# Two attention stages of a six-stage transformer kernel: first-block scores of four heads in one product, maxima added to the query rows on VectorE, and a shifted order of projection and value products

## The reference

```
x = x + 0.5 * L0_ffn(layernorm(x))      # 32 gated experts, 8 chosen, and a shared one
x = x + L0_attn(layernorm(x))           # "attn0": 16 heads of 8, causal softmax
x = x + 0.5 * L0_ffn(layernorm(x))
x = x + 0.5 * L1_ffn(layernorm(x))      # 8 experts of 512, 2 chosen
x = x + L1_attn(layernorm(x))           # "attn1": 16 heads of 8, relu scores / their sum
x = x + 0.5 * L1_ffn(layernorm(x))

# attn0, for each of 8 batches, S = 512, H = 16, HD = 8
scores  = einsum('bhqd,bhkd->bhqk', Q, K) / sqrt(8);  scores = where(k > q, -1e6, scores)
attn    = einsum('bhqk,bhkd->bhqd', softmax(scores), V) @ Wo + bo
# attn1, inside it a residual and a layer norm of its own
w       = relu(einsum('bhqd,bhkd->bhqk', q, k) / sqrt(8));  w = w / (sum(w) + 1e-6)
y       = x + einsum('bhqk,bhkd->bhqd', w, v) @ w_out + b_out;  out = layernorm(y)*gamma + beta
```

## Time and profile before

| | |
|---|---|
| median of 3 runs | 2064.63 us (2064.27 to 2064.72) |
| profiled execution | 2066.3 us, its span 2064.3 us |
| busy over the span | PE 1985.8 us (96%), DVE 1632.7 (79%), ACT 1200.7 (58%), POOL 930.1 (45%) |
| chain that ended last, by engine | PE 64%, DVE 11%, issue 11%, POOL 9%, ACT 3% |
| attn0 | first exponential at 347.8, last at 707.6 us; a loop chunk 45.78 us |
| attn1 | first scores at 1416.4, last at 1677.4 us; loop chunks 31.9 to 34.7 us |

### The profile page before, as it was taken

One profiled execution on the slowest core, in us unless ns is written; L12 is line 12 of the kernel. 1 busy time (PEld: TensorE's weight loads), 2 busy tenths in 40 slices (PEclk: granted clock), 3 DMA queues, 4 the chain that ended last, 5 costly groups with the idle time before them and its releaser, 6 DMA issues.

```text
span 2064.3 us, 44740 instructions
## 1 busy us (share of the span) xinstructions
PE 1985.8 (96%) x10752; PEld 1438.8 (70%) x10752; DVE 1632.7 (79%) x3337; ACT 1200.7 (58%) x1736; POOL 930.1 (45%) x904
## 2 busy tenths in 40 slices
PE   6999998999999999999999999998999999999998
PEld 4777776666666677777877888874333357787787
DVE  7777777777777577777588888886777788888887
ACT  6667664555555577676554445445767764454544
POOL 4665663333332366666544444442122334444444
PEclk9999999999999999999999999999999999999999
DMA  6333343333232243444311111114233301111112
GB/s 210 101 122 113 108 120 112 98 97 96 82 91 82 55 130 118 130 129 114 112 37 47 41 46 46 45 43 138 84 130 104 120 28 46 47 46 41 41 51 72
DMA packets 120701, 179.29 MB, mean 87 GB/s; under 512 B 33840, under 2 KB 38576, under 8 KB 120496
## 3 DMA queue, kind: packets, MB, share of 16 engines
q1 hardware_dynamic: 120624, 178.37, 29.3%
HBM read 147.10 MB, written 31.20 MB: 86 GB/s over the span
## 4 chain that ended last, share of the span: by engine, by line
PE 64%; DVE 11%; issue 11%; POOL 9%; ACT 3%; DVEq 1%; POOLq 1%; DMA 0%; SPq 0%; ACTq 0%
PE pair L397 14%; PE pair L399 13%; PE pair L398 13%; POOL h_lo L1364 6%; PE bank L651 5%; PE pair L740 3%; PE bank L629 3%; PE pair L762 3%; PE pair L823 2%; PE bank L397 2%; PE bank L399 1%; PE bank L398 1%; DVE rmax L1188 1%; DVE h_hi L1131 1%; POOL rstd L1284 1%
## 5 line engine op out<-in xcount | busy, mean ns | idle before, releaser
L1370 POOL TENSOR_TENSOR h_lo<-hid,h_hi 128x512 fp32r<-128x512 f32 x256 | 335.5, 1311 | 410.4 <-ACT h_hi L920 410.1
L397 PE MATMUL pair<-xnT_hi,w_hi 128*128 (+1 forms) x1040 | 420.0, 404 | 2.6 <-DVE prod L1110 1.3
L1364 POOL TENSOR_TENSOR h_lo<-hid,h_hi 128x512 fp32r<-128x512 f32 x256 | 332.3, 1300 | 194.6 <-ACT h_hi L886 193.4
L399 PE MATMUL pair<-xnT_hi,w_lo 128*128 (+1 forms) x1040 | 407.7, 392 | 0.0
L398 PE MATMUL pair<-xnT_lo,w_hi 128*128 (+1 forms) x1040 | 407.4, 392 | 0.0
L915 ACT ACTIVATE hid<-pair,bias 128x512 f32<-128x512 f32 x256 | 176.6, 690 | 315.5 <-PE pair L399 273.8
L397 PE MATMUL pair<-h_hi,w_hi 128*128 128x512 f32 x784 | 311.5, 397 | 14.5 <-DVE h_lo L1133 6.2
L399 PE MATMUL pair<-h_hi,w_lo 128*128 128x512 f32 x784 | 306.5, 391 | 0.0
L398 PE MATMUL pair<-h_lo,w_hi 128*128 128x512 f32 x784 | 305.9, 390 | 0.0
L1131 DVE TENSOR_SCALAR h_hi<-pair,nb 128x512 fp32r<-128x512 f32 x256 | 191.2, 747 | 69.8 <-PE pair L399 67.1
L938 ACT ACTIVATE probs<-pair 128x1024 f32<-128x1024 f32 x160 | 163.5, 1025 | 130.2 <-PE pair L762 127.0
(11 more groups left out here) (164 smaller groups left out, 3234.4 us busy)
## 6 DMA issues: line engine op xcount, KB each, us to landing
wb<-parts_dram SPq DMA_DIRECT2D x512, 128.0 KB, 2.9
wb<-parts_dram SPq DMA_DIRECT2D x128, 256.0 KB, 3.3
parts_dram<-attn_parts SPq DMA_DIRECT2D x96, 256.0 KB, 2.9
attn_q_st<-parts_dram SPq DMA_DIRECT2D x64, 256.0 KB, 2.7
k_one<-parts_dram SPq DMA_DIRECT2D x128, 64.0 KB, 2.5
attn_k_st<-parts_dram SPq DMA_DIRECT2D x32, 256.0 KB, 3.0
stage_w<-in_w_dram SPq DMA_DIRECT2D x32, 130.0 KB, 2.4
stage_w<-in_w_dram SPq DMA_DIRECT2D x5, 512.0 KB, 6.6
```

What stands on the lines that cost most here:

```text
L397: eng.matmul(o, w_hi_, v_hi, start=start, stop=False, **kw)
L399: return eng.matmul(o, w_lo_, v_hi, start=False, stop=stop, **kw)
L1364: eng.tensor_tensor(h_lo[:, p % NH0, :], hid[:, unit_of(p) % NHID, :] if p else hs[:, :], h_hi[:, p % NH0, :].bitcast(F32), ALU.subtract). ...
L1370: eng.tensor_tensor(h_lo[:, j % NH1, :], hid[:, j // 2 % NHID, :], h_hi[:, j % NH1, :].bitcast(F32), ALU.subtract).then_inc(lo1p_ready, 1)
```

## The change

*attn0, TensorE.* Query block 0 leaves fills 2 and 3, which become two products of 384 columns with masks of 128. It gets a tile of its own half: `first_block_by_query` does the first block of all four heads in one product of 512 columns, with one mask of 512 columns. Fill 4 becomes two products of 512 columns (heads 0 and 2, heads 1 and 3) in place of four of 256. `maxima_to_rows` loses the identity product. It moves from before the scores by key of steps 4, 9, 14, 19 to behind everything in steps 3, 8, 13, 18, and the first-block product of the quad after follows it in the other bank of the same pair. USES changes with it, and so does who waits for which reader.

*attn0, VectorE and ScalarE.* Fills 2 and 3 need one reduction each in place of two, the first block one of 512 columns for each quad. `rows_to_stack` moves from ScalarE (a copy) to VectorE (an addition of the PSUM tile and q_st).

*attn1.* The three value products of the chunk before go to steps 0, 1 and 2, one each. "half" moves from step 2 to 3, "proj" from step 10 to 11, "xn_a" and "xn_b" from step 1 to 2.

```diff
-    ("attn1", "attn1"): ((2, "dve", "half"), (3, "dve", "fin"), (4, "act", "aT_hi"), (5, "dve", "aT_lo"), (10, "pe", "proj"),
+    ("attn1", "attn1"): ((3, "dve", "half"), (3, "dve", "fin"), (4, "act", "aT_hi"), (5, "dve", "aT_lo"), (11, "pe", "proj"),
...
-    "attn1": ((0, 0, 0, 1, 1, 3, 3, 4), (6, 6, 7, 7, 8, 8, 9, 9, 12, 14, 14)),
+    "attn1": ((0, 0, 0, 2, 2, 3, 3, 4), (6, 6, 7, 7, 8, 8, 9, 9, 12, 14, 14)),
...
-PV_AT = ((-3,), (-2, -1), (), (0, 1), ...
+PV_AT = ((-3,), (-2,), (-1,), (0, 1), ...
...
-Q_FILLS = ((0, ((3, 0),)), (1, ((3, 0),)), (0, ((2, 0), (0, 384))), (1, ((2, 0), (0, 384))), (None, ((1, 0),)))
+Q_FILLS = ((0, 3), (1, 3), (0, 2), (1, 2), (None, 1))
...
-MAX_AT = (4, 9, 14, 19)
+MAX_AT = (3, 8, 13, 18)
...
+        def first_block_by_query(eng, ch, quad, b):
+
+            o = pair[b][:, 1, :].rearrange("p (h s) -> p h s", s=P)
+            eng.matmul(o, mem0.q_st[:, quad, 0:P], mem0.k_one[:, quad, :, 0:P], start=True, stop=True, skip_group_check=True)
+            eng.matmul(o, identb, neg.unsqueeze(1).broadcast_to([P, QUAD, P]), start=False, stop=True, skip_group_check=True).then_inc(s0_ready, 1)
+
         def maxima_to_rows(eng, ch, quad, b):
 
             eng.wait_ge(neg_max.sem, 2 * (NQ * ch.g + quad + 1))
-            eng.matmul(pair[b][:, 0, :], ident_r[:, :], mem0.q_st[:, quad, :], start=True, stop=False, skip_group_check=True)
             for t in range(NT):
...
-            elif len(Q_FILLS[fill][1]) == 1:
-                eng.tensor_reduce(q[:, 3, heads], src[:, :, :], AX_X, ALU.max).then_inc(s_used, 1)
             else:
-                eng.tensor_reduce(q[:, 2, heads], src[:, :, 0:384], AX_X, ALU.max)
-                eng.tensor_reduce(q[:, 0, heads], src[:, :, 384:S], AX_X, ALU.max).then_inc(s_used, 1)
+                qt = Q_FILLS[fill][1]
+                eng.tensor_reduce(q[:, qt, heads], src[:, :, 0:(qt + 1) * P], AX_X, ALU.max).then_inc(s_used, 1)
...
+        def first_block_maximum(eng, ch, quad, b):
+
+            eng.wait_ge(s0_ready, NQ * ch.g + quad + 1)
+            eng.tensor_reduce(mem0.rmax[:, quad % 2, 0, :], pair[b][:, 1, :].rearrange("p (h s) -> p h s", s=P),
+                              AX_X, ALU.max).then_inc(s0_used, 1)
+
+        def rows_to_stack(eng, ch, quad, b):
+
+            eng.wait_ge(q_ps, NQ * ch.g + quad + 1)
+            eng.tensor_tensor(mem0.q_st[:, quad, :], pair[b][:, 0, :], mem0.q_st[:, quad, :].bitcast(F32), ALU.add).then_inc(q_full, 1)
```

77 lines of the change are left out of this document (48 added, 29 removed).

## The result

| | before | after |
|---|---|---|
| median (runs beside each other) | 2064.53 us, 4 runs | 2048.73 us, 4 runs (2046.0 to 2049.41) |
| ratio, 95% interval | | 0.9919 (0.9906 to 0.9933) |
| span of the profiled execution | 2064.3 us | 2046.2 us |
| attn0, first to last exponential | 359.85 us | 353.34 us |
| attn1, first to last scores | 260.99 us | 252.42 us |

The change is faster by 16 us. I had forecast 34 and a range of 2023 to 2046, so the sign is right and the size is twice too large.

The account below looks back on a forecast made before the run. TensorE was taken to set the pace in attn0 and be busiest in attn1, waiting there for readers of its score tiles. 2064.6 - 14 (attn0) - 13.5 (attn1) - 6 (attn1's clock) = 2031 us, range 2023 to 2046.

Parts of the forecast that it names:

- attn0, TensorE's work: attn0, each quad: fewer and shorter products and masks save TensorE 0.41 us, 13 us in 32 quads (bounds 2 to 20).
- attn0, VectorE's time: attn0 loop chunk: VectorE's work rises from 35.1 to 37.2 of about 44 us.
- the turn's wait: attn0, chunk head: TensorE's wait at the turn, 0.26 us by the record, grows to 0.8 to 1.0.
- attn0, waits: attn0: maxima's wait goes, VectorE catches up in steps 4, 9, 14; net -0.2 us a chunk, -1.6 in eight.
- the rival in which VectorE sets attn0's pace: attn0: TensorE waits for the addition and first block's reduction at 32 places; 43 us more, 2074 us; chance 0.04.
- My sign of being wrong: attn0 chunks staying above 45 us, meaning VectorE late in steps 18 to 3; or a 0.50 clock in attn0.
- attn0, the start: attn0's stage start, eight fills running ahead: VectorE's reductions and addition change by -1.2 and +2.0, so +0.8 us.
- attn1, steps 10 to 12: attn1: with step 10's scores ahead of the projection, TensorE's wait for ScalarE goes; -1.4 us a chunk.
- attn1, the sum over chunks: attn1: seven chunks at 1.9 us each, -13.5 us (range -8 to -16), with y_norm starting as before.
- the spread's gain: attn1, steps 1 to 4: xn ready in time, waits at the turn and step 3's scores go; -0.5 us a chunk.
- attn1, the last chunk: attn1's last chunk: counted among the seven chunks that each save 1.9 us.
- attn1, the clock: attn1: half-clock stretches go with the wait in steps 10 and 11, -6 us; rival that they stay, 2037 us, 0.12.

Follow-up runs that it names:

- half_between: Changed kernel with attn0's two VectorE groups half placed between the reduction of the fill by query and rows_to_stack with first_block_maximum; 2042.36 us, ratio 0.9885.
- rows_scalar: Changed kernel with the identity product ahead of the maxima's again and ScalarE's copy in place of VectorE's addition in attn0; 2048.22 us.
- proj_alone: Changed kernel keeping, of attn1's edits, only the projection behind step 10's scores; value products, half and xn as before the change; 2061.58 us.
- no_multiply: Changed kernel without GpSimd's multiplication in attn1's y_add, so it computes something else and serves for time alone; 2044.43 us.
- attn0_alone: Changed kernel with attn1's three tables (value products and half, projection, xn) as before the change; 2060.30 us.
- spread_alone: Changed kernel with attn1's projection back in step 10 ahead of its scores; value products' spread, half and xn stay as changed; 2056.99 us.
- mul_vector: Changed kernel with y_add's multiplication in attn1 moved from GpSimd to VectorE, behind y_scale, all work done; 2049.75 us.
- xn_step3: Changed kernel with attn1's xn and the turn, with its halves hi and lo, one step later; 2057.58 us.
- keep_step8: Changed kernel with attn1's kept copy on GpSimd in step 8, and a third buffer taken from 64 bytes a partition of padding ahead of the weights; 2066.49 us.

## Why the prediction was wrong in size

By the spans the change gave 18.1 us and I had summed 33.6. Point by point:

- **attn0, TensorE's work: a term mis-sized.** I had the pair of 384 columns at 0.35 from a line through products in a stream, and took it off 0.58, which was read where the group's first product starts late. In the chunk the eight pairs take 0.35 to 0.54, 0.455 in the mean, and the eight groups of four before 0.53 to 0.63, 0.60 in the mean: 0.14 saved a fill, not 0.23. Their masks went from 0.15 to 0.095, 0.055 saved and not 0.10. In favour came the identity product: it and the maxima took 0.72 and the maxima alone 0.45, 0.27 saved for 0.19. Fill 4 (0.47) and the first block with its mask (0.28, 0.04, and 0.10 that the next group's first product starts later: 0.42 for 0.45) are right. By these groups TensorE's work fell by 1.0 us a chunk, where I had 1.6: some 5 us in eight. With half_between the chunk is 44.3, at the upper end of the 43.5 to 44.3 that I had named, but partly by luck: work came out 0.6 short, and the waits other than L644's 0.2 better than forecast.
- **attn0, VectorE's time: right; the turn's wait: right.** 37.25 against 37.2; 0.92 by the starts against 0.8 to 1.0.
- **attn0, waits: the step that failed.** I wrote that in steps 4, 9 and 14 the 24 value products "give VectorE time to catch up". In 4 and 14 these products themselves wait for VectorE: half stands in its queue right behind rows_to_stack and the first block's reduction, which the change had just put there. I had costed the two as work, and not asked what is queued behind them on VectorE and who waits for that. 0.85 to 0.89 us a chunk, some 7 us in eight; half_between takes it back in full. It is near the rival in which VectorE sets attn0's pace, in two places of a chunk and not in four, and TensorE waits there for the turned value sums and not, as in that rival, for a pair. My sign of being wrong, chunks above 45 us, came true (45.17), but I had put the lateness into steps 18 to 3; it stood in 4 and 14.
- **attn0, the start.** I had +0.8; the time to the first exponential fell by 1.75. Executions with a half-clock stretch near 39 us (the kernel before's has one, the one after has none) have this time at 346.5 to 347.3 with the same work up to there, those without at 345.8 to 346.0. So about 1 of the 1.75 goes with that stretch, and some 0.8 is a gain of the other sign than forecast. rows_scalar, whose work up to there differs, has the stretch and 345.7, so this split is an estimate; no run took it apart.
- **attn1, steps 10 to 12: right where they stand.** Chunk 1 fell from 32.12 to 30.27, in proj_alone to 30.73.
- **attn1, the sum over chunks: the second step that failed.** "So it starts as before", I said of y_norm, and stopped there. y_norm starts a chain of 13 us (y_norm, y_rstd, y_scale, y_add, the copy, the next chunk's rstd, xn, the turn) that runs over the chunk's end. It starts 23.7 us into the chunk in place of 23.1, in a chunk that is 0.7 shorter: so it ends 1.3 later by the next chunk's clock, GpSimd's addition into x at +0.1 where it stood at -1.2. There the turn waited 0.38 us already. 0.95 us in each of five chunks (no_multiply), and the spread's gain is what remains of it: 0.7 a chunk in place of 1.9. Over chunks 1 to 6, 191.3 (six of 31.89) became 186.3, so 5.1 us of work against 11.4 forecast. (Seven times 1.9 is 13.3 and not the 13.5 that I had added.)
- **attn1, the last chunk.** I had counted 1.9 us there too; it became 2.7 longer. This chunk prepares the feed-forward stage, and ScalarE has the routing's work in steps 8 to 10; it stands idle for 2.44 us until VectorE has ended its part of the routing (L1082), with the relus of the scores queued behind. Before, the projection ahead of step 10's scores covered that. ScalarE's and TensorE's timelines after:
```profile
1645.75 0.23 ACT L877 ACTIVATE wgt<-sel 128x32 f32<-128x32 f32 x1 [2.44 <-DVE sel L1082]
```
```profile
1644.79 0.50 PE L850 MATMUL pair<-attn_q_st,attn_k_st 24*128 24x512 f32 x2
1646.94 0.50 PE L850 MATMUL pair<-attn_q_st,attn_k_st 24*128 24x512 f32 x2 [1.65 <-ACT probs L968]
```
  2.15 where such a pair of halves takes 0.43, and a microsecond later the clock falls. Its windows from there on:
```profile
1647.95:1654.78 6.83, 6.83 (x33) 2.55 (x32) 4.74 (x18) 3.73 (x4) 1.02 (x1) 0.50 0.00 1
```
  The runs bear out that the projection had covered it: with the projection in step 10 (attn0_alone, spread_alone) TensorE waits 0.17 ahead of half 21 and 0.50 ahead of half 23, as in the kernel before (0.16 and 0.51), and with it in step 11 (proj_alone and the changed kernel) 1.63 to 1.65 ahead of half 21. Not all of the 2.7 is this wait: the stretch behind it is of 6.83 us here, and in five of the eight profiled executions with these attn1 tables of 3.41 us, as in the kernel before; there the chunk takes 31.5, 1.2 longer than before. So about 1.2 is waiting and 1.5 a longer stretch in this execution.
- **attn1, the clock: right in chunks 1 to 6.** 197.5 less 191.3 is 6.2 us before, and no stretch after (forecast -6). Of the 6.2 the three chunks with a stretch have 5.7; chunks 1 and 6 took 32.1 at full clock. The reason was half right: it isn't step 11's wait alone, since proj_alone without it has three stretches and spread_alone with it five; with both edits there is none, though the turn waits 1.05 us. A single wait decides nothing either: mul_vector with 0.9 us more of it at step 0 has one stretch in six chunks, xn_step3 with 0.69 and 0.98 none.

Together, 15.5 us are missing by the spans. attn0's stage gave 6.5 for 14.6, so 8.1 are missing there: some 5 by the work, 7 by L644; against them the other waits came out nearly 2 better, and about 2 are luck of the clock, since the kernel before has two half-clock stretches near attn0's end (684.31 to 687.72, and from 704.79 on) and the one after has none. (The 2 is an estimate from attn0's last chunk: 42.50 in attn0_alone with a stretch from 690.91 on, 41.36 in proj_alone with one from 696.33 on, 40.87 without one.) attn1's stage gave 8.6 for 19.3: 6.3 of the missing in chunks 1 to 6 and 4.6 in the last one (1.9 and 2.7), with 0.2 back by the clock. The start (2.6) and the stretches between the stages (1.3) came out better. That makes 14.9; the rest is what I had rounded up in the sum.

## What to carry to other kernels

When work is added to an engine's queue, price not only the work: name the next instruction behind it that another engine waits for, and put the added work behind that one if its own reader is later (half_between: a reordering of three groups, 0.85 us in each attn0 chunk). A price that is read between the starts of two groups holds for the neighbours that it was read with: read a new group's price, and the old one's, behind the same kind of neighbour. When a step is moved later, or a loop's body gets shorter, follow what it starts over the loop's boundary to the first instruction of the other side that the busiest engine waits for. And look at the first and last turns of a loop apart from the others: what they prepare differs, and a step that is moved may have been covering something there.

## What the runs showed that I had not expected

- **A small tensor_scalar of VectorE is held back by a GpSimd addition.** L991 (128x4, from SBUF to SBUF) takes 0.17 us; it took 1.25, from 1503.04 to 1504.29, where GpSimd's copy ran from 1502.98 to 1504.26. L1176 took 0.97 for 0.19 beside the copy at 1519.42. Relus that read PSUM (L1268, 1.2 us) were not longer beside such additions. Both held rows end with GpSimd's, and L991 is so held in each of attn1's chunks 2 to 7 of the kernel after (1.25 to 1.30 us). So an addition on GpSimd costs more than its own time if such a row coincides with it. The Trainium skill (SBUF — State Buffer, SBUF: two separate sides) says that VectorE and GpSimd have one pair of SBUF ports in common, which one of them holds for a whole instruction while the other stands still; by that rule VectorE's rows are held back only if they run in a mode with two ports or have two inputs in SBUF. The rows agree so far as L991's end lies 0.03 us behind the copy's (1504.29 and 1504.26) and the relus that read PSUM kept their 1.2; in which mode L991 and L1176 run no row shows.
- **The address of the data counts.** 32 or 64 bytes a partition less padding ahead of the weights make the kernel 17 to 19 us slower (2066.25 and 2066.44 against 2047 to 2049, and the kernel before beside them 2064.4), with the same instructions: products of the feed-forward stages are further apart by 1 to 2%. Whoever needs a buffer has to find room without moving what TensorE reads, or measure the shift by itself first.
- **A step's number is not a time.** In keep_step8 a table entry moved from step 5 to step 8 changed nothing, since no wait lies between the two on GpSimd.
